# The low part of the last feature chunk is computed on GpSimd between its second and third bias, no longer on VectorE

## What is computed

```python
self_feat = concat([v, q]) @ W_self.T + b_self           # q is 0 for rows of v that sum to 0
output = self_feat
for d in range(2):                                       # both directions of the edges
    A = (adj, adj transposed)[d][:, :, :20]
    cond, vb = A.sum(-1), A @ w_bias + b_bias
    kv = self_feat[:, :20]
    aff = (self_feat @ Wq.T + bq) . (kv @ Wk.T + bk)     # 16 heads of 32
    aff = where(cond > 0, aff / sqrt(32), -9e15) + vb
    w = softmax(aff)
    output += (w @ kv) @ Wout + bout                     # per head
return v + relu(output)
```

## Time and profile before

| what | value |
|---|---|
| median of three runs | 644.89 us |
| the profiled execution's own time | 645.47 us |
| its span | 643.5 us |
| mean granted clock of TensorE, of full | 0.961 |
| TensorE busy | 604.0 us, 94% |
| VectorE busy | 480.6 us, 75% |
| GpSimd busy | 435.2 us, 68% |
| ScalarE busy | 413.1 us, 64% |

### The profile page before, as it was taken

How to read it: one execution, slowest core, us unless ns; L and a number is a source line. 1 busy time by engine, 2 the same in 40 slices (tenths; PEclk the granted TensorE clock), 3 DMA queues, 4 the chain that set the end, 5 groups by cost and what they waited for, 6 DMA issues and landing times.

```text
span 643.5 us, 11289 instructions
## 1 busy us (share of the span) xinstructions
PE 604.0 (94%) x4303; PEld 503.2 (78%) x4303; DVE 480.6 (75%) x652; ACT 413.1 (64%) x829; POOL 435.2 (68%) x386
## 2 busy tenths in 40 slices
PE   9999999999898999989899998989998989999891
PEld 6977888879687788869698886868887877888570
DVE  4896688788777788687787867687887777776681
ACT  5566737968466587757487773758775665866240
POOL 0402499848779676878787695868588796768551
PEclk9999999999889899989899997989999998999797
DMA  9975352564728464664736384754638483741406
GB/s 325 410 285 142 71 163 87 160 169 149 219 86 252 90 188 147 201 173 166 189 130 187 68 244 119 214 145 128 197 109 249 112 237 77 216 133 32 122 5 197
DMA packets 42867, 106.05 MB, mean 165 GB/s; under 512 B 12478, under 2 KB 26302, under 8 KB 36414
## 3 DMA queue, kind: packets, MB, share of 16 engines
q1 hardware_dynamic: 40654, 89.61, 42.6%
q0 software_dynamic: 2160, 15.73, 12.9%
HBM read 85.84 MB, written 19.47 MB: 164 GB/s over the span
## 4 chain that ended last, share of the span: by engine, by line
PE 83%; DVE 10%; POOL 2%; ACT 2%; issue 1%; DVEq 0%; ACTq 0%
PE aff L580 31%; PE gen L511 9%; PE gen L512 9%; PE gen L513 9%; PE aff L547 7%; DVE sfl L977 7%; PE gen L640 4%; PE tp L594 3%; PE gen L650 3%; PE tp L511 1%; ACT z L765 1%; POOL z L1272 1%; PE tp L512 1%; PE tp L513 1%; PE tp L413 1%; DVE wol L1098 1%
## 5 line engine op out<-in xcount | busy, mean ns | idle before, releaser
L1272 POOL TENSOR_TENSOR z<-z,mx 128x640 f32<-128x640 f32 x63 | 86.9, 1380 | 84.2 <-DVE mx L1029 83.9
L580 PE MATMUL aff<-gh,sfh 128*128 128x320 f32 x504 | 120.1, 320 | 23.8 <-DVE sfl L977 23.8
L879 ACT ACTIVATE z<-z 128x640 f32<-128x640 f32 x63 | 46.6, 739 | 124.4 <-POOL z L1272 123.6
L580 PEld LDWEIGHTS aff<-gh,sfh 128*128 128x128 f32 x504 | 84.2, 191 | 43.0 <-issue 42.9
L580 PE MATMUL aff<-gh,sfl 128*128 128x320 f32 x504 | 116.8, 313 | 0.0
L580 PE MATMUL aff<-gl,sfh 128*128 128x320 f32 x504 | 116.5, 313 | 0.0
L1260 POOL TENSOR_TENSOR z<-cb,bx 128x640 f32<-128x640 f32 x64 | 100.4, 1708 | 11.1 <-PE tp L513 10.2
L511 PE MATMUL gen<-xh,w1h 128*128 128x512 f32 x256 | 104.3, 407 | 0.1
L513 PE MATMUL gen<-xh,w1l 128*128 128x512 f32 x256 | 101.2, 395 | 0.0
L512 PE MATMUL gen<-xl,w1h 128*128 128x512 f32 x256 | 101.2, 395 | 0.0
L1257 POOL TENSOR_TENSOR sfl<-sff,sfh 128x512 fp32r<-128x512 f32 x48 | 64.8, 1487 | 43.1 <-ACT sfh L746 43.1
(11 more groups left out here) (158 smaller groups left out, 1180.0 us busy)
## 6 DMA issues: line engine op xcount, KB each, us to landing
x<-in_x SPq DMA_DIRECT2D x16, 1024.0 KB, 7.0
xn<-in_xn SPq DMA_DIRECT2D x31, 512.0 KB, 5.4
sff<-in_x POOLq DMA_DIRECT2D x15, 1024.0 KB, 8.4
out_y<-sff SPq DMA_DIRECT2D x15, 1024.0 KB, 3.9
msk<-in_mask SPq DMA_DIRECT2D x16, 880.0 KB, 7.1
cb<-c_scratch SPq DMA_DIRECT2D x16, 320.0 KB, 4.4
nz<-nz_scratch SPq DMA_DIRECT2D x16, 256.0 KB, 4.8
wkT<-in_wkT SPq DMA_DIRECT2D x4, 512.0 KB, 7.9
```

The lines of the kernel that those rows point to most:

```text
L580: mm = nc.tensor.matmul(aff[:, t % 2, half, 0:SH], s, g[:, b - starts[group(b)], f, half * SH:(half + 1) * SH], start=(f == 0 and i == 0), ...
L1272: nc.gpsimd.tensor_tensor(zt(slot, t), zt(slot, t), heads(mx, t, M), ALU.subtract).then_inc(s_sub, 1)
```

## The change

VectorE keeps the low part of chunk 3 for batch 0 alone. For all the other batches GpSimd makes it, after the biases of tiles 0 and 1 and before those of tiles 2 and 3. The waits are counted anew: from batch 1 on GpSimd makes all four chunks of a batch, so that the count is `n * FC - FL + f + 1` of the one semaphore `s_sfl2` (FC = 4, FL = 1).

```diff
+        def sf_lows(n, f):
+            if n == 0:
+                return (s_sfl2, f + 1) if f < FC - FL else (s_sfl, FL)
+            return s_sfl2, n * FC - FL + f + 1
...
             # TensorE, scores
-                        if t == 0 and f < FC - FL:
-                            pe.wait_ge(s_sfl2, b * (FC - FL) + (f + 1))
-                        elif t == 0:
-                            pe.wait_ge(s_sfl, b * FL + FL)
+                        if t == 0:
+                            pe.wait_ge(*sf_lows(b, f))
...
             # ScalarE, add_bosum (last batch)
-                    act.wait_ge(s_sfl2, (b + 1) * (FC - FL))
-                    act.wait_ge(s_sfl, (b + 1) * FL)
+                    act.wait_ge(*sf_lows(b, FC - 1))
...
             # VectorE: the function is left for batch 0 alone, and its calls
             # in first_batch and batch are gone
-            def sf_low(n, slot):
-                dve.wait_ge(s_sfh, n * FC + FC)
-                nc.vector.tensor_tensor(sfl[:, FC - 1, :], sff[n % 3][:, FC - 1, :], sfh[:, FC - 1, :].bitcast(F32),
-                                        ALU.subtract).then_inc(s_sfl, 1)
+            def first_sf_low():
+                dve.wait_ge(s_sfh, FC)
+                nc.vector.tensor_tensor(sfl[:, FC - 1, :], sff[0][:, FC - 1, :], sfh[:, FC - 1, :].bitcast(F32), ALU.subtract).then_inc(s_sfl, 1)
...
                 add_query(n, other, FC - 1)
-                sf_low(n, other)
                 nonzero(n + 1, True)
...
             # GpSimd, batch
-                    for t in range(T):
-                        bias(n, other, t)
+                    bias(n, other, 0)
+                    bias(n, other, 1)
+                    sf_low(n, other, FC - 1)
+                    bias(n, other, 2)
+                    bias(n, other, 3)
                     sub_max(n, other, 0)
```

More of the change, by code:

```diff
@@ L1161, in _ @@
             g_low(0, 7)
-            sf_low(0, 0)
+            first_sf_low()
             def x_low(n, c):
```

## The result

The changed kernel takes 627.21 us, median of four runs (626.60 to 627.38), beside 644.01 us for the kernel before (641.87 to 646.11): a ratio of 0.9738, 95% interval 0.9702 to 0.9773. It is 2.6% faster. The profiled execution took 627.11 us, with a span of 625.0, against 645.47 and 643.5 before: 18.4 us less, where 26.9 were forecast.

What follows compares the result with a forecast made beforehand. TensorE bounds the kernel, waiting 23.8 us in nine bodies for VectorE's held subtraction. Pairs 20.6, clock in second bodies 3.1, last body 3.9, less 0.7: 26.9 us off, giving 618.0; own range 611 to 625, with rivals 603 to 629.

Steps and rivals of the forecast that it cites:

- A: Rival: VectorE is let in at the next boundary between GpSimd instructions, so `nonzero` is short; 37.0 us gained, 607.9; chance 0.33.
- B: Rival: GpSimd can't be pressed, its 2.9 us of idleness stay; 10.6 us gained, 634.3; chance 0.12.
- the 2.3 us of the subtraction: Ordinary bodies: with chunk 3's low part on GpSimd, TensorE goes on 2.3 us earlier, leaving a wait of 0.35 us.
- The clock, 1.56 us: TensorE's stretch to tile 1's scores: clock stays up, saving 1.56 us in first bodies; half, 0.8, taken in second ones.
- nonzero held to the end of the run: VectorE in ordinary bodies: `nonzero` waits until GpSimd's run ends, about 6.4 us on record; second shift 0.8 us late.
- The second ordinary body: Second body of a pair: TensorE released at 312.0 instead of 316.5, waiting 1.3 us; 4.5 or 5.8 us saved per pair.
- pressed, it needs the 17.0: GpSimd from `sub_max` to its next low part: 17.0 us of work in 19.89, shrinking to 17.0 when pressed.
- Still 0: Five group bodies: even if `nonzero` is held to 358.9, the first shift comes before TensorE needs it; 0 us lost.
- The last ordinary body: Body n = 15, alone and with no `nonzero` behind it on VectorE: 3.9 us saved.
- Body b = 0: First body, where VectorE was let in after 0.8 us: GpSimd's low part ends later, 0.7 us lost once.
- rival C: Slower: the transposes wait 2.7 us for the last normalising and the clock may fall; +11 us, 656; chance 0.04.
- The rule against the change: GpSimd has about half VectorE's speed for two-input operations; by this alone every batch would lose some 0.6 us.

Runs made afterwards that it cites:

- e4: The kernel before with 15 additional, never-read matmuls ahead of TensorE's wait for the low part of chunk 3 in the nine ordinary bodies: 628.06 us, ratio 0.9767.
- e3: The changed kernel with `nonzero` in its old place as a reduction, the comparison with zero left out: 608.12 us, ratio 0.9463.
- e12: The changed kernel with `nonzero` as the same comparison in a form that also writes a sum nobody reads: 608.75 us, ratio 0.9463.
- e6b: The changed kernel with GpSimd's accumulating DMA issued earlier, ahead of the normalising of tile 2, behind a wait long over: 602.57 us, ratio 0.9363.
- e1: The changed kernel with `nonzero` moved behind `label_mask` and the first shift on VectorE in every body: 610.19 us, ratio 0.9494.
- e13: The kernel before, subtraction still on VectorE, with GpSimd's accumulating DMA issued ahead of the normalising of tile 2: 600.95 us, ratio 0.9322.

## Why the prediction was right, and where it was off

The median of 627.21 us lies in the stated range of 603 to 629, but 9.2 us above the forecast and outside the 611 to 625 that the forecast gave for itself. The path was largely right. That the wide range held the result is luck in part: it was drawn wide for A and B, not for the step that cost most.

- **What bounded the kernel, and the 2.3 us of the subtraction: right.** TensorE is released 0.35 us after it wants the low part, as forecast, in each first ordinary body.
- **The clock, 1.56 us: right in the first bodies, and in the second ones right in the sum by luck.** I took half for a wait of 1.3 us. The waits were 1.8 us; behind two of the four the clock fell to 0.64 and behind two it stayed in full, so the half is right in no body by itself. What decides between the two stays open. e4 and the trace of the kernel before put the clock at 15 to 17 of the some 41 us that the old waits cost.
- **nonzero held to the end of the run: right**, 6.48 us where about 6.4 were forecast. Rival A came out at 608 us, and e3 and e12 measure 608.1 and 608.8 when the hold is taken away. Where the hold is really passed on at the next boundary, which is A's mechanism, e6b measures 602.6, so A's number is met in part by chance.
- **The second ordinary body: too good by about 1 us.** The step that failed is "pressed, it needs the 17.0". From `sub_max` to the next low parts GpSimd took 17.94 us with 16.90 of work; about 1 us of its waiting for VectorE stayed. The rest was right: 6.44 us from the release to `sub_max` (6.6 forecast) and 8.46 on to the next release (8.44). From one release to the next it gained 34.17 - (309.83 - 276.99) = 1.3 us where 2.2 were forecast, and the other three pairs fell short by as much (0.8 to 0.9 us).
- **The group bodies: the step that cost most.** "Still 0" was argued for `nonzero` and the first shift of that body alone. What came in was the lateness of the body before: VectorE's sum behind ScalarE's exponential, the split of g behind the sum, and the key products behind the split, a chain that the prediction did not follow. From the second release of a pair to the next first one, before 311.50 + 4.83 + 0.15 = 316.48 to 389.15, after 309.83 to 381.39, it gained 1.1 us. Forecast were the 2.3 of the release and the half of the clock, 3.1. Three such stretches gained 1.2, 1.1 and 1.2 us, about 2 less each, which is nearly 6 of the 8.5 us that are missing. They took 71.5 or 71.6 us whether the clock had fallen behind the second release or not: TensorE's own speed was not what set them. The fourth gained 2.6. e1 puts 16 to 17 us on the whole of the hold.
- **The last ordinary body** gave 1.4 us more than forecast: its stretch to tile 1 had taken 5.84 us in the kernel before, at a clock of 0.50, not the 4.70 of the earlier trace rows.
- **Body b = 0**: 0.67 us of wait for the low part, 0.7 forecast. **The new waits in the transposes** (rival C) came, 0.4 us in each of four bodies and not 2.7. The prediction named any such wait as a sign of being wrong. It cost nothing: TensorE waited for the low part afterwards in any case.
- **Rival B** fell: GpSimd could be pressed, up to 1 us. **The rule against the change**, GpSimd's lower speed, shows in b = 0, where the low part came 0.7 us late, and in no group body, where nothing waited for it. And e13 shows that the rule had a point: unhindered, VectorE does as well.

Not asked by the prediction at all was why VectorE is kept out of a whole run. It used that difference to choose between two values, and did not ask whether one could change it.

## What to carry to other kernels

When a small VectorE instruction is on record for microseconds beside GpSimd, don't ask first which engine should have it; ask what lets it in, because the next instruction of the same kind takes its place in the queue. Follow the lateness of an engine's list into the next body as well as through the present one, and price an idle stretch of TensorE with the slower matmuls behind it. A DMA issued by GpSimd wants a place that isn't just ahead of a run that another engine has to get past.

## What the runs showed of the hardware

- Behind its accumulating DMA GpSimd's instructions were on record 0.3 us into each other, and then VectorE's two-input subtraction and its plain comparison from SBUF were kept out across two, four and five boundaries between them (4.8, 6.5, 8.0 us). Without that overlap they were let in at the next boundary (0.35 to 1.5 us). Moving the DMA, with a wait ahead of it that was long over, switches between the two (e6b, e13). Inside the overlap the Trainium skill's account in SBUF (Who interferes with whom), blocked until the other's instruction is over, falls short; outside it it agrees. In the traces the overlap lasts until GpSimd has to wait for something; that was not tried by a run of its own.
- A comparison of 4 columns in the form that also writes a sum (0.15 us, and 0.08 us to read the sum), or a reduction, ran unhindered in the same place.
- After 2.64 us of idleness TensorE's granted clock fell to 0.50 to 0.66 of full for the next stretch, in nine of nine bodies. After 1.8 us it fell to 0.64 in two of four, after 2.0 us in the one case of e6b (302.72), and after 0.35 and 0.67 us it stayed in full.
